# A GRU recurrence on one core: gate inputs written into PSUM by ScalarE, and TensorE's products of a step reordered

## The reference

```python
def cell(h, x):
    gi = x @ W_ih + b_ih
    gh = h @ W_hh + b_hh
    i_r, i_z, i_n = jnp.split(gi, 3, axis=-1)
    h_r, h_z, h_n = jnp.split(gh, 3, axis=-1)
    r = jax.nn.sigmoid(i_r + h_r)
    z = jax.nn.sigmoid(i_z + h_z)
    n = jnp.tanh(i_n + r * h_n)
    h_new = (1.0 - z) * n + z * h
    return (h_new, h_new)
```

## Time and profile before

| | |
|---|---|
| median of 3 runs | 4073.15 us (4071.14 to 4074.32) |
| span of the profiled execution | 4078.2 us, 5.05 above that median; no other time of it is given |
| busy share of the span | PE 91%, PEld 68%, DVE 67%, ACT 51%, POOL 12% |
| busiest lines | L1521 and L1511, the calls of `high` and `low` |

### The profile page before, as it was taken

The page is one execution under the profiler, slowest core; times in us unless marked ns, Lnnn a source line. Parts: engine busy times, 40 slices in busy tenths (PEclk is TensorE's granted clock), DMA queues, the critical chain, the costliest instruction groups (busy, mean ns, idle before and its releaser), DMA issues. The chain is left out here.

```text
span 4078.2 us, 177223 instructions
## 1 busy us (share of the span) xinstructions
PE 3719.3 (91%) x70140; PEld 2792.5 (68%) x70140; DVE 2749.4 (67%) x10621; ACT 2082.2 (51%) x7371; POOL 478.1 (12%) x411
## 2 busy tenths in 40 slices
PE   2458888888999999999999998999999999999999
PEld 2425465554699999999999996565456546644664
DVE  8878788786677777777777776576367537653763
ACT  4028678677755555555555553453245315532542
POOL 2006366364000000000000000001000100010001
PEclk9979999998755555555555556999999999999999
DMA  2023132231000000000000003211221141023102
GB/s 93 1 89 94 48 110 87 60 106 56 4 6 6 6 6 6 6 6 6 6 6 6 6 6 137 83 41 42 109 90 34 42 158 52 23 83 124 44 14 93
DMA packets 113888, 203.31 MB, mean 50 GB/s; under 512 B 44076, under 2 KB 76844, under 8 KB 111416
## 3 DMA queue, kind: packets, MB, share of 16 engines
q1 hardware_dynamic: 113720, 201.00, 14.8%
HBM read 160.05 MB, written 32.52 MB: 47 GB/s over the span
## 5 line engine op out<-in xcount | busy, mean ns | idle before, releaser
L1521 PE MATMUL gru_sum_n<-gru_state_parts,w_hh_hi 128*128 128x8 f16 x8192 | 499.6, 174 | 0.0
L1511 PE MATMUL gru_sum_n<-gru_state_parts,w_hh_lo 128*128 128x4 f16 x8192 | 488.9, 168 | 0.0
L1511 PEld LDWEIGHTS gru_sum_n<-gru_state_parts,w_hh_lo 128*128 128x128 f16 x8192 | 376.5, 104 | 0.0
L1521 PEld LDWEIGHTS gru_sum_n<-gru_state_parts,w_hh_hi 128*128 128x128 f16 x8192 | 376.5, 104 | 0.0
L653 ACT ACTIVATE dit_prob<-dit_bank,dit_head_nbias 128x512 f32<-128x512 f32 x256 | 175.9, 687 | 351.0 <-DVE dit_head_nbias L671 350.6
L1654 DVE TENSOR_TENSOR_SCAN gru_n_in<-gru_reset_gate,gru_sum_n 128x32 f32<-128x32 f32 x1024 | 225.4, 220 | 54.7
L1511 PE MATMUL gru_sum_rb<-gru_state_parts,w_hh_lo 128*128 128x4 f16 x4096 | 261.3, 168 | 0.0
L1521 PE MATMUL gru_sum_za<-gru_state_parts,w_hh_hi 128*128 128x8 f16 x4096 | 254.1, 169 | 0.0
L1521 PE MATMUL gru_sum_ra<-gru_state_parts,w_hh_hi 128*128 128x8 f16 x4096 | 254.1, 168 | 0.0
L1521 PE MATMUL gru_sum_zb<-gru_state_parts,w_hh_hi 128*128 128x8 f16 x4096 | 254.1, 168 | 0.0
L1511 PE MATMUL gru_sum_zb<-gru_state_parts,w_hh_lo 128*128 128x4 f16 x4096 | 252.1, 166 | 0.0
(11 more groups left out here) (335 smaller groups left out, 12378.5 us busy)
## 6 DMA issues: line engine op xcount, KB each, us to landing
dit_w_qk<-w_qk_parts SPq DMA_DIRECT2D x64, 512.0 KB, 3.6
room<-w_parts SPq DMA_DIRECT2D x8, 4096.0 KB, 12.8
room<-w_v_parts SPq DMA_DIRECT2D x5, 4096.0 KB, 12.2
room<-w_out_parts SPq DMA_DIRECT2D x4, 4096.0 KB, 14.8
small_given_w<-in_L_cond_qkv_w SPq DMA_DIRECT2D x48, 256.0 KB, 3.1
w_qk_parts<-small_parts_w SPq DMA_DIRECT2D x32, 256.0 KB, 2.1
small_given_w<-in_L_cond_ffn_w SPq DMA_DIRECT2D x32, 256.0 KB, 3.7
w_parts<-small_parts_w SPq DMA_DIRECT2D x32, 256.0 KB, 2.4
```

Source lines behind the costliest of these rows:

```text
L1511: mm = pe.matmul(columns[:, j, 0], w_hh[1][:, k, c:c + P], parts[:, par, 0, k, :, LAST], start=opens, stop=False, skip_group_check=True)
L1521: mm = pe.matmul(columns[:, j], w_hh[0][:, k, c:c + P], parts[:, par, :, k, :, LAST], start=opens, stop=False, skip_group_check=True)
```

## The change

- The four calls of `bring`, `gi_now`, its DMAs and semaphores go. Four matmuls with zeros open the banks once, before the loop; no matmul on them has `start=True` afterwards.
- ScalarE writes the inputs of step i + 1 into the banks during step i: `seed(i + 1, 0)` into ra and za behind `keep` of half a, `seed(i + 1, 1)` into rb and zb behind `keep` of half b. Each writes 2 x 16 columns, in two banks.
- `copy_gi_n` for the next step moves from behind `keep` of half a to behind `seed(i + 1, 1)`.
- TensorE's 24 calls of a step stand in another order, with waits for `seeded_a` and `seeded_b` and with `gn_ready` before the third call.
- SP's loads into `room` wait for the last seed.

```diff
@@ -1430,11 +1430,9 @@
...
-        scaled_ident = m.sb("scaled_ident", [P, P], F16)
...
+        zero_columns = m.sb("gru_zeros", [P, HALF * 2 * B], F16)
...
@@ -1444,7 +1442,8 @@
...
-        ra_bank, rb_bank, za_bank, zb_bank = (m.ps(s, [P, 4 * P]) for s in ("sum_ra", "sum_rb", "sum_za", "sum_zb"))
+        gate_banks = m.ps("sum_rz", [P, 2, 2, 4 * P])
+        ra_bank, za_bank, rb_bank, zb_bank = (gate_banks[:, half, gate] for half in range(2) for gate in range(2))
...
@@ -1470,15 +1468,7 @@
...
-            for v in range(2):
-                sp.dma_start(gi_now[v][:], gi_rz[:, v * NOW:(v + 1) * NOW]).then_inc(now_loaded[v], 16)
-            with sp.Fori(0, T // (2 * NOW) - 1) as n:
-                for v in range(2):
-                    sp.wait_ge(now_taken[v], n + 1)
-                    sp.dma_start(gi_now[v][:], gi_rz[:, at(n * (2 * NOW) + (2 + v) * NOW, NOW)])\
-                      .then_inc(now_loaded[v], 16)
-            for v in range(2):
-                sp.wait_ge(now_loaded[v], 16 * (T // (2 * NOW)))
+            sp.wait_ge(seeded_b, T)
             sp.dma_start(region[1], store.out.rearrange("p e k n -> p e (k n)")).then_inc(first_loaded, 16)
...
@@ -1489,12 +1479,6 @@
...
-            def bring(bank, gate, fs, v, o):
-
-                return pe.matmul(bank[:, 0:HALF * 2 * B], scaled_ident[:],
-                                 gi_now[v][:, o, gate, fs[0]:fs[-1] + 1].rearrange("p f e b -> p (f e b)"),
-                                 start=True, stop=False, skip_group_check=True)
...
@@ -1525,50 +1509,44 @@
...
-            with pe.Fori(0, T // (2 * NOW)) as n:
-                for s in range(2 * NOW):
-                    i, par, v, o = n * (2 * NOW) + s, s % 2, s // NOW, s % NOW
+            for bank in (ra_bank, za_bank, rb_bank, zb_bank):
+                mm = pe.matmul(bank[:, 0:HALF * 2 * B], const["ident16"][:], zero_columns[:], start=True, stop=False,
+                               skip_group_check=True)
+            mm.then_inc(banks_opened, 1)
+            with pe.Fori(0, T // TURN) as n:
+                for s in range(TURN):
+                    i, par = n * TURN + s, s % 2
                     na, nb = new_columns(par, 0), new_columns(par, 1)
 
-                    pe.wait_ge(z_in_a, i + 1)
-                    if o == 0:
-                        pe.wait_ge(now_loaded[v], n * 16 + 16)
-                    bring(za_bank, Z_GATE, first, v, o)
-                    pe.wait_ge(r_in_a, i + 1)
-                    bring(ra_bank, R_GATE, first, v, o)
-                    pe.wait_ge(r_in_b, i + 1)
-                    bring(rb_bank, R_GATE, second, v, o)
-                    pe.wait_ge(z_in_b, i + 1)
-                    mm = bring(zb_bank, Z_GATE, second, v, o)
-                    if o == NOW - 1:
-                        mm.then_inc(now_taken[v], 1)
+                    pe.wait_ge(seeded_a, i + 1)
                     pe.wait_ge(hi_a, i + 1)
-                    low(rb, R_GATE, second, first, par)
+                    low(ra, R_GATE, first, first, par)
                     low(za, Z_GATE, first, first, par)
-                    low(ra, R_GATE, first, first, par)
-                    low(zb, Z_GATE, second, first, par)
                     pe.wait_ge(gn_ready, i + 1)
                     low(na, N_GATE, first, first, par, opens=True)
+                    pe.wait_ge(seeded_b, i + 1)
+                    low(zb, Z_GATE, second, first, par)
                     pe.wait_ge(lo_a, i + 1)
+                    high(ra, R_GATE, first, first, par)
+                    high(rb, R_GATE, second, first, par)
+                    high(na, N_GATE, first, first, par)
                     high(za, Z_GATE, first, first, par)
-                    high(na, N_GATE, first, first, par)
-                    high(ra, R_GATE, first, first, par)
                     pe.wait_ge(hi_b, i + 1)
+                    low(za, Z_GATE, first, second, par)
+                    low(rb, R_GATE, second, first, par)
                     low(ra, R_GATE, first, second, par)
-                    high(zb, Z_GATE, second, first, par)
-                    low(za, Z_GATE, first, second, par)
                     pe.wait_ge(lo_b, i + 1)
                     high(ra, R_GATE, first, second, par).then_inc(ra_sum, 1)
-                    high(na, N_GATE, first, second, par)
                     high(za, Z_GATE, first, second, par).then_inc(za_sum, 1)
+                    low(na, N_GATE, first, second, par)
+                    high(na, N_GATE, first, second, par).then_inc(na_sum, 1)
+                    high(zb, Z_GATE, second, first, par)
                     low(rb, R_GATE, second, second, par)
-                    low(na, N_GATE, first, second, par).then_inc(na_sum, 1)
-                    high(zb, Z_GATE, second, second, par)
-                    high(rb, R_GATE, second, first, par)
                     high(rb, R_GATE, second, second, par).then_inc(rb_sum, 1)
-                    low(zb, Z_GATE, second, second, par).then_inc(zb_sum, 1)
-                    high(nb, N_GATE, second, second, par, opens=True)
-                    low(nb, N_GATE, second, second, par)
+                    low(zb, Z_GATE, second, second, par)
+                    high(zb, Z_GATE, second, second, par).then_inc(zb_sum, 1)
+                    low(nb, N_GATE, second, second, par, opens=True)
+                    high(nb, N_GATE, second, second, par)
                     high(nb, N_GATE, second, first, par)
                     low(nb, N_GATE, second, first, par).then_inc(nb_sum, 1)
...
@@ -1591,41 +1569,56 @@
...
+            def seed(i, half):
+
+                act.activation(gate_banks[:, half, :, 0:HALF * 2 * B],
+                               gi_rz[:, at(i), :, half * HALF:(half + 1) * HALF].rearrange("p o g k e b -> p (o g) (k e b)"),
+                               ACT.Copy, scale=GS / GIS).then_inc((seeded_a, seeded_b)[half], 1)
+
+            def step(i, par, more):
...
+                act.activation(keep[:, A, :, LAST], z_in[:, A], ACT.Sigmoid, scale=-1.0 / GS).then_inc(keep_a, 1)
+                if more:
+                    seed(i + 1, 0)
+                act.wait_ge(n_in_a, i + 1)
+                act.activation(mix[:, A, :, 0], n_in[:, A, :, GATED], ACT.Tanh, scale=1.0 / GS).then_inc(n_a, 1)
...
+                act.activation(keep[:, Z, :, LAST], z_in[:, Z], ACT.Sigmoid, scale=-1.0 / GS).then_inc(keep_b, 1)
+                if more:
+                    seed(i + 1, 1)
+                    copy_gi_n(i + 1, 1 - par)
+                act.wait_ge(n_in_b, i + 1)
+                act.activation(mix[:, Z, :, 0], n_in[:, Z, :, GATED], ACT.Tanh, scale=1.0 / GS).then_inc(n_b, 1)
...
             act.wait_ge(made, 1)
+            act.wait_ge(banks_opened, 1)
+            seed(0, 0)
+            seed(0, 1)
             copy_gi_n(0, 0)
-            with act.Fori(0, T // 2) as pair:
+            with act.Fori(0, T // 2 - 1) as pair:
...
-                    act.activation(keep[:, A, :, LAST], z_in[:, A], ACT.Sigmoid, scale=-1.0 / GS).then_inc(keep_a, 1)
-                    copy_gi_n(i + 1, 1 - par)
-                    act.wait_ge(n_in_a, i + 1)
...
-                    act.activation(keep[:, Z, :, LAST], z_in[:, Z], ACT.Sigmoid, scale=-1.0 / GS).then_inc(keep_b, 1)
-                    act.wait_ge(n_in_b, i + 1)
...
+                    step(pair * 2 + par, par, True)
+            for par in range(2):
+                step(T - 2 + par, par, par == 0)
...
-            dve.tensor_scalar(scaled_ident[:], const["ident16"][:], GS / GIS, None, ALU.mult)
+            dve.memset(zero_columns[:], 0.0)
...
```

More of the change, by code:

```diff
@@ L1432, in gru_phase @@
         ones = m.sb("gru_ones", [P, B])
-        scaled_ident = m.sb("scaled_ident", [P, P], F16)
-        NOW = 2
-        gi_now = [m.sb(f"gi_now_{v}", [P, NOW, 2, KD, 2, B], F16) for v in range(2)]
+        zero_columns = m.sb("gru_zeros", [P, HALF * 2 * B], F16)
+        TURN = 4
         LAST, GATED = 2, 3
@@ L1460, in gru_phase @@
         gn_ready, kept = m.sem("gn_ready"), m.sem("history_kept")
-        now_loaded = [m.sem(f"gi_now_loaded_{v}") for v in range(2)]
-        now_taken = [m.sem(f"gi_now_taken_{v}") for v in range(2)]
+        banks_opened, seeded_a, seeded_b = m.sem("banks_opened"), m.sem("seeded_a"), m.sem("seeded_b")
         back_turned, added, stored = m.sem("back_turned"), m.sem("added"), m.sem("gru_stored")
@@ L1643, in _ @@
             dve.engine_nop().then_inc(made, 1)
-            for s in (r_in_a, r_in_b, z_in_a, z_in_b):
-                dve.sem_inc(s, 1)
             def total(out, bank):
```

30 lines of the change are left out of this document (13 added, 17 removed).

## The result

The median of four runs is 4144.34 us (4140.35 to 4147.08), beside 4073.74 us (4071.14 to 4074.61) for four runs of the kernel before. The ratio is 1.0171, 95% interval 1.0156 to 1.0185: slower by 70.6. The forecast was 4140, +67, in a range of 4103 to 4170.

The account below looks back on a forecast made before the run. A ring through three engines sets the step (2.769); with the change a ring over ScalarE does, at 2.88. Profiled span 4078.2 + 57 + 9 + 1 = 4145; the median lies 5 below the span, so 4140, range 4103 to 4170.

Parts of the forecast that it names:

- Part 4: ScalarE's copy for gate n, moved behind its second half, stalls TensorE before group 3: step 2.88, +57.
- the ring over ScalarE: Loop from TensorE's group 3 over z's reduction, sigmoid, keep, seed and copy back to group 3: 2.88 a step.
- Part 1: Four matmuls leave TensorE: only the excess at a turn's end goes, 0.02 a step if the ring stays the bound.
- the state ring: Loop through TensorE, VectorE and ScalarE by the new state: 2.75 a step before, 2.76 with the change.
- Part 2: The n sum comes one TensorE group earlier, so VectorE's scan for n starts sooner: 0.04 a step taken back.
- Part 3: TensorE's first group waits for two semaphores, seeded_a and hi_a: +0.05 a step, between 0 and 0.09.
- "Faster" rival: No bound at gn_ready and TensorE's double wait free: ring 2.71, 4052; chance 0.07.
- Part 5: The two 4 MB loads into room start later, with nothing behind the recurrence to hide it: +9, between 0 and 9.
- The +1 for the start: At the start, four opening matmuls and three ACTIVATEs stand before the first group: +1.
- the one without a bound at `gn_ready`: ScalarE's small instructions pass faster than their rows, TensorE's wait is no bound: 4078; chance 0.08.
- the dear seed: ScalarE's seed over two PSUM banks doesn't overlap, 0.20 for 0.11: step 3.00, 4201; chance 0.08.
- the rise of the clock: TensorE goes to the 2.4 GHz level in the recurrence: at best -435; chance 0.02.

Follow-up runs that it names:

- e1: The changed kernel with TensorE's third and fourth groups exchanged, so the wait for gn_ready comes one group later: 4094.9 us, ratio 1.0047.
- e3: The changed kernel with ScalarE's copy for gate n moved from behind the second seed to behind the tanh of half a: 4091.8 us, ratio 1.0043.
- e4: The changed kernel with one more ACTIVATE of 8 elements a partition between the second seed and the copy: 4197.9 us, ratio 1.0298.
- e5: The changed kernel with one more ACTIVATE of 8 elements a partition behind the tanh of half a: 4146.7 us, ratio 1.0174.
- e11: e9 with the order of the kernel before from the sixth group on, na_sum on group 16 again: 4074.6 us, ratio 1.0002.
- e9: e6 with the call low on rb, first blocks, moved from tenth to fifth, so lo_a is wanted at group 6: 4054.6 us, ratio 0.9950.
- e6: e3 with TensorE's two waits in front of group 1 in the other order: 4070.7 us, ratio 0.9984.
- e7: The kernel before with only TensorE's 24 calls in the order of the change: 4067.9 us, ratio 0.998.
- e10: The kernel before with its two 4 MB loads into room held back until the history of the step before the last: 4086.7 us, ratio 1.0031.
- e2: The changed kernel with TensorE's two waits in front of group 1 in the other order: 4143.6 us, ratio 1.0175.

## Why the prediction was right

**Part 4, the ring over ScalarE**, forecast 2.88 from eight terms: measured 2.883. The terms were within 0.01 each: 0.11 for the seed's slot, the one with no row, measured 0.119 in nanoseconds' resolution (1504.38 to 1504.49 above), and sigmoid to `keep` 0.115 for 0.11. e1, e3 and e4 confirm the ring from three sides: TensorE wants the copy later, ScalarE makes it sooner, and something is added to the ring; e5 adds the same off the ring, for nothing. +57 was forecast, +58.2 is in the trace. Here the Trainium skill (ScalarE: Activation LUTs, What ACT_TABLE_LOAD costs) would have put some 20 on top, as an estimate; the seed's slot agrees with the 0.12 worked out from it, but the copy of 16 elements takes 0.17 and not 0.20. The agreement is luck: by the same page of the Trainium skill, as an estimate, the seed would take 0.21 and overlap by 0.09, and in the trace it takes 0.18 and overlaps by 0.06.

**Part 1**, forecast as 0.02 a step behind the state ring: e11 shows just that. The four matmuls that the change takes off TensorE are worth 12 in 4074, since TensorE waited anyway in three steps of four.

**Part 2**, forecast -0.04: -0.038 by e9 and e11, and 0.46 for 0.50 to the scan in the trace. The prediction had the n sum and the sigmoid arrive together; the semaphores put the n sum 0.03 ahead (0.402 and 0.432 into a step of the kernel before). But its wait is an instruction of its own on VectorE's queue, which ends at 0.451, behind the sigmoid, and the scan starts at 0.494. With the change it ends at 0.350, and the scan starts at 0.455.

**Part 3** was forecast as +0.05, between 0 and 0.09. It is 0.067: e3 with the late wait written second has a step of 2.775, e9 with it written first 2.708, and neither stalls elsewhere. With part 2 that is, up to rounding, 2.747 (e11) - 0.038 + 0.067 = 2.775 for the state ring, where the forecast had 2.76. The term was 0.017 too small, and nothing came of it, since the ring over ScalarE was the longer one.

**What the "Faster" rival left out** is `lo_a`. That the wait costs nothing "behind the stall" was right for the changed kernel; but the rival has no stall, and there it costs 0.025 at group 5 (e6 against e9). So its 2.71 needed one more edit than a free double wait. The forecast was not touched, but e6 and e7, whose sums left it out too, came out 11 and 8 above them.

**Part 5** was forecast as +9: 8.5 in the trace, and e10 shows it one for one (10.3 for 10.3). The +1 for the start was too much: from the semaphore `made`, behind which ScalarE (before) or TensorE (after) may start, to the first reduction it is 2.17, where it was 1.92.

**The sum** came out at 4145 for the profiled span and 4140 for the median, by taking off the 5 by which the shown profile lay over its median. The median is 4144.3. By steps the trace gives (2.883 - 2.769) x 512 = 58.4, and 8.5 more, 66.9; 3.7 of the 70.6 remain. By the same sum, each with its own steps and its own time to the next phase, 1.1 (e2) to 6.2 (e4) remain for the other kernels with seeds, 3.7 on average; of the two without, e7 leaves 0.4 and e10 2.7. From the next phase's start to the end the traces with seeds take 1553.8 to 1557.5, and those without 1552.0 to 1554.4, 2.7 less on average. What causes this isn't settled.

The rivals: the one without a bound at `gn_ready` (4078) and the dear seed (4201) are excluded by the step of 2.883, and the rise of the clock by the granted 0.50. The faster one came true as a kernel of its own, with the step of 2.71 in e9, but only after three edits: the copy early, as its condition said, the two waits exchanged, since the double wait was not free, and the group moved for `lo_a`.
